# Twelve gate values of an LSTM step side by side in PSUM, in place of 28 and 112 words apart

## The reference, cut to what matters

```python
def step(carry, xs):
    h, c = carry
    xi_t, xf_t, xg_t, xo_t = xs                  # x @ U + b for every gate
    i_t = jax.nn.sigmoid(xi_t + h @ V_i)
    g_t = jnp.tanh(xg_t + h @ V_c)
    o_t = jax.nn.sigmoid(xo_t + h @ V_o)
    c_new = h * c + i_t * g_t                     # the forget gate is computed and not used
    h_new = o_t * jnp.tanh(c_new)
    return ((h_new, c_new), h_new)
```

## Time and profile before

| | |
|---|---|
| Time, median of 3 runs | 3998.58 us |
| Time of the profiled execution | 4001.42 us |
| Its span, first to last instruction | 3999.7 us |
| Recurrence, first to last read of the gates | 200.1 to 3994.4 us |
| TensorE busy | 3587.6 us (90%) |
| VectorE / ScalarE / GpSimd busy | 85% / 63% / 54% |
| TensorE granted clock, mean | 0.523 |

### The profile page before, as it was taken

How to read it: one execution, slowest core, us unless ns; L and a number is a source line. 1 busy time by engine, 2 the same in 40 slices (tenths; PEclk the granted TensorE clock), 3 DMA queues, 4 the chain that set the end, 5 groups by cost and what they waited for, 6 DMA issues and landing times.

```text
span 3999.7 us, 130354 instructions
## 1 busy us (share of the span) xinstructions
PE 3587.6 (90%) x35548; PEld 2661.6 (67%) x35548; DVE 3382.5 (85%) x21828; ACT 2527.8 (63%) x11666; POOL 2153.8 (54%) x3173
## 2 busy tenths in 40 slices
PE   6899998989899999999999999999989899988887
PEld 5666666666666666666666666666666666666665
DVE  6788888888888888888888888888888888887787
ACT  3366666666666666666666666666666666666565
POOL 6656565655565656555555556555655565652222
PEclk9955555555555555555555555555555555555555
DMA  5000000000000000000000000000000000000000
GB/s 74 2 2 1 1 1 1 1 1 1 1 1 1 1 1 1 1 1 1 1 1 1 1 1 1 1 1 1 1 1 1 1 1 1 1 2 1 1 1 1
DMA packets 44537, 11.06 MB, mean 3 GB/s; under 512 B 39913, under 2 KB 44010, under 8 KB 44490
## 3 DMA queue, kind: packets, MB, share of 16 engines
q1 hardware_dynamic: 42378, 10.05, 1.6%
q10 hardware_dynamic: 2112, 0.46, 0.1%
HBM read 7.29 MB, written 3.21 MB: 3 GB/s over the span
## 4 chain that ended last, share of the span: by engine, by line
PE 66%; DVE 14%; ACT 13%; issue 5%; POOL 1%; DVEq 0%; DMA 0%; ACTq 0%; POOLq 0%
PE GATES L1342 14%; PE YB L1162 10%; PE GATES L1412 9%; ACT O L736 7%; PE H1B L1156 7%; ACT G L732 6%; DVE O L985 6%; PE YB L1313 6%; PE TAPB L1149 6%; PE DB L1281 5%; DVE HR L989 5%; PE DB L1143 3%; PE H2B L1189 1%; PE H1B L1189 1%; PE H2B L1137 1%
## 5 line engine op out<-in xcount | busy, mean ns | idle before, releaser
L732 ACT ACTIVATE G<-GATES 128x12 f32<-128x12 f32 x3136 | 572.5, 183 | 1206.1 <-PE GATES L1412 1194.6
L1412 PEld LDWEIGHTS GATES<-HR,VW 128*128 128x128 f16 x6272 | 419.5, 106 | 603.4 <-issue 557.7
L1342 PE MATMUL GATES<-HR,VW 128*128 128x4 f16 x3136 | 531.6, 170 | 308.3 <-DVE HR L989 214.5
L977 DVE TENSOR_TENSOR_SCAN CT<-G,CT 128x12 f32<-128x12 f32 x3136 | 587.5, 187 | 246.9 <-ACT G L732 217.9
L736 ACT ACTIVATE O<-G 128x8 f32<-128x8 f32 x3136 | 662.8, 211 | 99.6 <-ACT G L732 0.2
L985 DVE RECIPROCAL O<-O 128x4 f32<-128x4 f32 x3136 | 567.9, 181 | 177.6 <-ACT O L736 0.7
L1408 PEld LDWEIGHTS <-VW 128*128 128x128 f16 x3136 | 457.8, 146 | 354.1 <-issue 317.5
L964 DVE SCALAR_TENSOR_TENSOR CT<-HIST,CT 128x4 f32<-128x4 f32 x3136 | 521.6, 166 | 126.7 <-DVE HIST L995 13.0
L1412 PE MATMUL GATES<-H,VB 128*128 128x4 f16 x6272 | 616.8, 169 | 0.0
L1412 PE MATMUL GATES<-HR,VW 128*128 128x4 f16 x6272 | 613.3, 168 | 0.0
L1162 PE MATMUL YB<-HD,W 128*64 128x112 f32 x3840 | 596.0, 412 | 2.1 <-DVE HD L857 2.1
(11 more groups left out here) (242 smaller groups left out, 6998.0 us busy)
## 6 DMA issues: line engine op xcount, KB each, us to landing
out_dram<-OUT SPq DMA_DIRECT2D x112, 28.0 KB, 1.9
X<-in_x_dram SPq DMA_DIRECT2D x4, 672.0 KB, 11.3
STG<-in_L_ffn_w_dram SPq DMA_DIRECT2D x4, 512.0 KB, 12.6
U<-in_L_conv_U2s_dram SPq DMA_DIRECT2D x1, 972.0 KB
W<-in_L_ffn_w_dram SPq DMA_DIRECT2D x1, 512.0 KB, 11.8
X<-in_x_dram ACTq DMA_DIRECT2D x4, 112.0 KB, 3.2
S<-in_L_conv_S1s_dram SPq DMA_DIRECT2D x1, 108.0 KB
S<-in_L_conv_S2s_dram SPq DMA_DIRECT2D x1, 108.0 KB
```

The costliest lines, as they stand in the source:

```text
L732: act.activation(G6[:, :, 2:5], gates[c][:, w, :, :], ACT.Tanh, scale=1 / GSCALE).then_inc(step_in, 1)
L977: dve.tensor_tensor_scan(CELL.rearrange("z b k -> z (b k)"), G6[:, :, :].rearrange("z b k -> z (b k)")[:, 0::2], ADD3.rearrange("z b k -> ...
L1342: return pe.add_instruction(mybir.InstMatmult(name=nc.get_next_instruction_name(), engine=mybir.EngineType.PE, start_tensor_calc=False, st ...
L1412: last = pe.matmul(gates[c][:, w, :, SLOT[g]], wt[:, g].rearrange("z m c -> z (m c)"), digit, start=False, stop=True, skip_group_check=True)
```

## The change

The twelve values of step t stood in a bank at column `k*112 + b*28 + t` for gate slot k and image b. Now they stand at `t*12 + b*3 + k`. Three views of the same 336 words change: the one of the steps (`gates`, written by the six matmuls, read by L732), and the two outputs in `prefill`. No instruction is added, removed or moved on any engine, and each has the same number of elements as before. The order of columns in which a prefill matmul produces its 112 results is the same; where they land differs: bias matmuls from 112 adjacent words to 112 words three apart, U x matmuls from four runs of 28 adjacent words to 28 words twelve apart, four times over. A step's matmul writes 4 words that were 28 apart and are now 3 apart, and L732 reads 12 adjacent words.

```diff
-        gates = [g[:, 0:HALF * B * 3].rearrange("z (k b t) -> z t b k", b=B, k=3) for g in GATES]
+
+        gates = [g[:, 0:HALF * B * 3].rearrange("z (t b k) -> z t b k", b=B, k=3) for g in GATES]
@@ prefill
-                return pe.matmul(GATES[c][:, SLOT[k] * TOK:(SLOT[k] + 1) * TOK], BX[:, k].rearrange("z m c -> z (m c)"),
+                return pe.matmul(GATES[c][:, 0:3 * TOK].rearrange("z (n k) -> z n k", k=3)[:, :, SLOT[k]], BX[:, k].rearrange("z m c -> z (m c)"),
                                  ONEH[:, :], start=(k == 0), stop=False, skip_group_check=True)
...
-            return pe.matmul(GATES[c][:, SLOT[g] * TOK:(SLOT[g] + 1) * TOK].rearrange("z (q p t) -> z p q t", q=Q, p=2),
+            return pe.matmul(GATES[c][:, 0:3 * TOK].rearrange("z (t q p k) -> z p q t k", q=Q, p=2, k=3)[:, :, :, :, SLOT[g]],
```

## The result

The changed kernel takes 4016.38 us (median of five runs, 4016.29 to 4026.41) against 3997.67 for the kernel before beside it: a ratio of 1.0050, 95% interval 1.0039 to 1.0062. Run again on another occasion it took 4017.19 against 3999.37, ratio 1.0043 (1.0029 to 1.0057). So it is slower by 18 to 19 us. The forecast of no visible difference was wrong. The time lies close to where rival B, a slower prefill, put it (4019).

The account below looks back on a forecast made before the run. The prediction took the recurrence loop's latency as the bound in 53 of 56 places. From 3998.6 us it took 3.9 off for the gate read and 0 for small matmuls and prefill: 3995, no visible difference, range 3976 to 4023.

Parts of the forecast that it names:

- rival B: Prefill gets slower, showing at place 6; 4019 us at the upper bound; chance 0.21 together with the small matmuls' unknown.
- The bound: The recurrence loop's latency sets the time in 53 of 56 places, about 1.21 us a turn, not TensorE's work.
- place 6: Row place held by TensorE's throughput at 1.22 us; doubled prefill matmuls would add 0.37 us a row, 20.9 us.
- The read of the gates: L732's read once a step, on the loop: 1.3 ns less from adjacent words, 3.9 us off in all.
- Rival C: Nothing at all changes: ScalarE walks word by word, the read stays at 182.6 ns; 3998.6 us; chance 0.24.
- rival A: The gate read gets markedly faster, up to 6.6 ns each; 3979 us at full gain, typically 3985; chance 0.25.
- The small matmuls: Six four-column matmuls of each step, on the loop; output words moving closer were taken to cost 0.
- The prefill: Nine 112-column matmuls for each bank and row, into scattered words: taken as 0 more, at most twice 93 ns.
- the unknown of the small matmuls: Successive matmuls of one step write neighbouring words; a cost would show from 2.7 ns a step; chance shared, 0.21.
- Place 51: Three prefill matmuls, 0.28 us more at the upper bound, against slack 0.14 + 0.08: 0.06 a row, 3.4 us.
- places 52 and 53: Two prefill matmuls each, 0.19 us more at the upper bound, within the slack before the experts' output: nothing.
- Place 3: Five prefill matmuls, 0.47 us more at the upper bound, within a slack of 0.59: nothing.

Follow-up runs that it names:

- the spread prefill: Changed kernel with prefill matmuls moved to places where TensorE has room (51 to 55, and 3, 6, 7): 4000.32 against 3999.42 us for the kernel before.
- second profile: Profile from running the changed kernel once more, unedited, beside the kernel before: 4017.19 us against 3999.37, ratio 1.0043.
- the pairs from an even and from an odd column: Kernel before with bias matmuls writing adjacent word pairs 56 apart: 3999.07 us; same with the gate area moved one column: 4009.86; against 3999.42.
- the empty place 6: Kernel before with the four prefill matmuls of place 6 put at place 7: 3999.22 against 3999.37 us, ratio 0.9999.

## Why the prediction was wrong

*The bound: right, but for place 6.* In 53 of 56 places the loop's latency sets the time, and TensorE's share of 90% says nothing of that. The kernel with the spread prefill shows it best: its prefill matmuls are as slow as in the changed kernel, and it takes the time of the kernel before. I had put place 6 to TensorE's throughput, and that was wrong (below).

*The read of the gates: wrong by a little.* I took 1.3 ns off, 3.9 us in all, from reads of other sizes (L786, L623). It is 0. Rival C had it right for this part, and rival A, with a chance of 0.25, falls: the read took 572.5 us in both layouts, and 224 scattered words took the 352 ns of adjacent ones.

*The small matmuls: right*, 0.

*The prefill: this is the step that failed.* I wrote "Upper bound: each word costs a cycle more than now, so twice 93 ns. I take 0", with the reason that TensorE's clock is at half here and the words come slowly. The upper bound was the truth: 187 ns. The reason doesn't hold: a lower clock doesn't hide the price, and the time of a matmul doubles at either clock. It does so too in the head rows, where the profile shows the full granted clock (1.00 from 160 to 175 us before and from 155 to 166 us in the changed kernel). Before, six U x matmuls:

```profile
169.09 0.46 PE L1132 MATMUL GATES<-X4S,UX 128*128 128x112 f16 x6
```

and in the changed kernel (second profile):

```profile
165.18 0.78 PE L1133 MATMUL GATES<-X4S,UX 128*128 128x112 f16 x6
```

The five steps between six starts went from (0.46 - 0.21) / 5 = 0.05 to (0.78 - 0.30) / 5 = 0.096, with 0.21 and 0.30 the durations of the last one (the minima of the tile view). The Trainium skill had the rule that decided, in "Advanced Engine Details and Errata", PSUM Cachelines: 8-byte lines, and every two consecutive elements should be contiguous. The trace agrees: 93 against 187 ns, and the pairs from an even and from an odd column, 298 against 475, show both the two words and the alignment. The wider wording that I had cited, that any pattern which isn't contiguous slows matmuls, doesn't hold here: pairs 56 words apart kept the 298 ns of one run. I gave rival B, together with the unknown of the small matmuls, a chance of 0.21, since no row could test it. That was too little: "no row shows it" is no evidence against a rule that speaks of just this pattern.

*The places: the sum nearly right, its parts not.* For the doubled matmul I had 24.3 us, against 19.0 from the four places. Place 6 was priced at 0.37 a row and cost 0.113. I took its 1.22 for a sign that TensorE held it, and the empty place 6 shows that it did not. The rest of the error has two parts. First, I counted four matmuls at 0.093 more each, but the distance from the first to the second hardly grew (0.05 to 0.06), so the convolution starts only 0.29 later. Second, there was room behind it. These are the convolution's second matmul in the kernel before and in the changed kernel (second profile):

```profile
1968.50 0.42 PE L1313 MATMUL YB<-N,WC 128*128 x1
```

```profile
1973.72 0.42 PE L1314 MATMUL YB<-N,WC 128*128 x1
```

It started 0.40 ahead of the next step's first matmul before (1968.90), and starts 0.21 ahead of it now (1973.94): the 0.19 between was room that I had not seen. So the step's first matmul comes 0.09 later after the read of the gates than before. The other 0.02 arise among the step's six matmuls: the second now starts 0.07 behind the first, and was 0.02 behind it.

Place 51 was priced at 0.06 and cost 0.20. I had counted two slacks, 0.14 between the last prefill matmul and the experts' output and 0.08 behind that. The first was none. The read of the gates in place 51 before was this:

```profile
2022.45 0.18 ACT L732 ACTIVATE G<-GATES 128x12 f32<-128x12 f32 x1 [0.16 <-PE GATES L1412]
```

The output started 0.19 after it (2022.64 in the earlier trace rows) and starts 0.47 after it now (2027.97 - 2027.50), the full 0.28 later. Only the 0.08 behind it was room. Why the output keeps that distance from the last prefill matmul wasn't tried. In places 52 and 53, priced at nothing, the output also moves by all that the two matmuls lengthened, 0.187; the room behind it is larger there, 0.17, as the output starts 0.09 earlier in the place, and each cost 0.013. Place 3, with five of the matmuls, had its room as read: 0.

*The rivals.* B happened, at 4016 to 4017 against its 4019. Its mechanism, a prefill at half the pace, is what the runs show; its place is not, since it looked to place 6, which has 6.4 of the 19.0 us, while place 51 has 11.2. That the number came out so near is luck: place 6 was priced too high and place 51 too low, and the 4019 holds a gain of 3.9 us on the read that never came.

## What to carry to other kernels

Lay out a PSUM tile for the matmul that writes many columns into it, so that it writes aligned pairs of fp32 words. The reads by ScalarE (12 and 224 words) took the same time in either layout, and a matmul of four columns showed nothing. Before a stream gets longer, find out how late an engine could still be in its place. A gap in front of an instruction need not be room: the one in front of the experts' output moved along in full. And a place that is longer than its neighbours isn't for that reason held by the busiest engine. When a slower stream can't be avoided, moving it to places with room can cost nothing, as the spread prefill did.

## What the runs showed of the hardware that I had not expected

From start to start, a matmul of 112 columns into scattered words takes 187 ns at 1.2 GHz (place 6) and 96 ns at 2.4 GHz (head rows), where into adjacent words it takes 93 and 49. The distance of the words made no difference: two, three and twelve apart all have a median duration of 475 ns. Pairs 56 words apart are as fast as a run of 112 (298 ns), if they start at an even column. With a column shift of one, matmuls in runs of 28 went from 93 to 100 ns from start to start. On ScalarE a scattered read of 224 words out of PSUM costs what an adjacent one does, 352 ns.
